# Both mixes of a tile behind the first step of the recurrence, in a kernel of four layers on one core

## The reference

```python
a_t = jnp.tanh(a)
def step(state, x_t):
    state = jnp.tanh(jnp.einsum('bhs,hst->bht', state, a_t) + jnp.einsum('bhd,hds->bhs', x_t, b))
    mixed = jnp.einsum('bhs,hsd->bhd', state, c) + skip[None] * x_t
    return (state, mixed)
...
return tokens + outs @ w_out.T + b_out
```

## Time and profile before

| | |
|---|---|
| median of 3 runs | 2249.52 us (2249.39 to 2250.3) |
| profiled execution: its own time | 2245.83 us |
| profiled execution: span | 2244.1 us |
| PE busy | 2186.6 us, 97% of the span |
| DVE, POOL, ACT busy | 1718.1, 1192.8, 1060.2 us |
| mean granted PE clock | 0.993 |

### The profile page before, as it was taken

The page is one execution under the profiler, slowest core; times in us unless marked ns, Lnnn a source line. Parts: engine busy times, 40 slices in busy tenths (PEclk is TensorE's granted clock), DMA queues, the critical chain, the costliest instruction groups (busy, mean ns, idle before and its releaser), DMA issues.

```text
span 2244.1 us, 92167 instructions
## 1 busy us (share of the span) xinstructions
PE 2186.6 (97%) x37362; PEld 1540.2 (69%) x37362; DVE 1718.1 (77%) x4980; ACT 1060.2 (47%) x2707; POOL 1192.8 (53%) x1680
## 2 busy tenths in 40 slices
PE   9999999999999999999999999998999999999997
PEld 5566565656556555556777777777888888887775
DVE  5788888888887777769999999994555555556997
ACT  4655665656666665552222222222444444443444
POOL 4555555655655555536666666674344444442334
PEclk9999999999999999999999999998999999999999
DMA  4111111211121111111210101100011111111232
GB/s 150 58 49 58 67 63 63 67 58 58 67 67 58 68 58 58 50 52 31 68 33 30 33 31 32 42 24 29 28 33 36 34 33 33 37 49 38 87 94 76
DMA packets 101634, 117.83 MB, mean 53 GB/s; under 512 B 10672, under 2 KB 80080, under 8 KB 101456
## 3 DMA queue, kind: packets, MB, share of 16 engines
q1 hardware_dynamic: 101456, 115.44, 15.8%
HBM read 48.29 MB, written 33.55 MB: 36 GB/s over the span
## 4 chain that ended last, share of the span: by engine, by line
PE 92%; DVE 4%; issue 2%; ACT 1%; POOL 0%; DVEq 0%; ACTq 0%; POOLq 0%
PE ps_state L1734 10%; PE ps_down L1373 7%; PE ps_gate L1366 7%; PE ps_up L1366 7%; PE ps_near L812 6%; PE ps_far L592 5%; PE ps_near L584 5%; PE ps_far L584 4%; PE ps_near L592 3%; PE ps_far L627 3%; PE ps_far L611 3%; PE ps_far L604 3%; PE ps_state L1765 3%; PE ps_state L1737 2%; PE ps_r L2152 2%; PE ps_v L2163 2%
## 5 line engine op out<-in xcount | busy, mean ns | idle before, releaser
L1616 ACT ACTIVATE r_state<-ps_state 128x64 f32<-128x64 f32 x1024 | 228.4, 223 | 288.7 <-PE ps_state L1737 283.9
L1734 PE MATMUL ps_state<-r_state,later_pairs_a 64*64 64x32 f32 x8192 | 338.3, 219 | 24.4 <-ACT r_state L1616 11.7
L1734 PEld LDWEIGHTS ps_state<-r_state,later_pairs_a 64*64 64x64 f32 x8192 | 298.2, 135 | 76.1 <-issue 56.3
L1737 PE MATMUL ps_state<-r_state,later_pairs_a 64*64 64x32 f32 x8192 | 334.8, 220 | 1.2 <-issue 1.1
L480 DVE CUSTOM_DVE_ANT_0 ps_near<-ps_near,mask 128x512 f32<-128x512 f32 (+1 forms) x512 | 270.4, 589 | 83.6 <-PE ps_near L584 83.5
L340 POOL TENSOR_SCALAR_AFFINE_SELECT probsT<-probsT 128x512 f32<-128x512 f32 x256 | 160.6, 640 | 266.1 <-ACT probsT L460 168.2
L1737 PEld LDWEIGHTS ps_state<-r_state,later_pairs_a 64*64 64x64 f32 x8192 | 289.7, 135 | 0.4 <-issue 0.4
L480 DVE CUSTOM_DVE_ANT_0 ps_far<-ps_far,mask 128x384 f32<-128x384 f32 (+1 forms) x512 | 198.3, 457 | 33.6 <-PE ps_far L584 32.5
L1256 POOL TENSOR_TENSOR f_fp<-f_rounded,f_scale 128x960 f32<-128x960 f32 (+2 forms) x67 | 117.3, 1751 | 162.7 <-DVE f_rounded L1345 162.7
L1278 ACT ACTIVATE f_silu<-ps_gate 128x704 f32<-128x704 f32 x64 | 48.4, 757 | 285.8 <-PE ps_gate L1366 285.8
L592 PE MATMUL ps_far<-Q,K 32*128 32x256 f32 (+2 forms) x1536 | 181.2, 416 | 1.2 <-ACT probsT L457 0.5
(11 more groups left out here) (218 smaller groups left out, 5411.7 us busy)
## 6 DMA issues: line engine op xcount, KB each, us to landing
q_swap<-q_sin SPq DMA_DIRECT2D x128, 128.0 KB, 2.1
k_swap<-k_sin SPq DMA_DIRECT2D x128, 128.0 KB, 2.1
xT<-in_xT_dram SPq DMA_DIRECT2D x16, 512.0 KB, 3.7
xtok<-in_x_dram SPq DMA_DIRECT2D x16, 512.0 KB, 3.8
x_rows<-x SPq DMA_DIRECT2D x16, 512.0 KB, 2.9
f_x<-x_rows SPq DMA_DIRECT2D x64, 128.0 KB, 2.1
x_rows<-f_x SPq DMA_DIRECT2D x64, 128.0 KB, 1.8
r_x<-x_rows SPq DMA_DIRECT2D x64, 128.0 KB, 2.1
```

The source lines that it names most:

```text
L1616: nc.scalar.activation(state[:, j % 2, banks, :, t, 0, :], sums[j % 2][:, banks, :, now], ACT.Tanh).then_inc(state_ready[t], 1)
L1734: nc.tensor.matmul(sums[j % 2][half(v), stays, c, now], A[half(v), 3 * q, c, :], last[half(v), stays, c, :], start=False, stop=True, skip_ ...
L1737: out = nc.tensor.matmul(sums[j % 2][half(1 - v), changes, c, now], A[half(v), 3 * q + 1 + was, c, :], last[half(v), changes, c, :], start ...
```

## The change

The table of places has one place for the mixes instead of two. Behind the recurrence of place 1 both mixes are issued, c = 0 and then c = 1; behind that of place 3 nothing is issued. The waits of the first mix stay ahead of both, and each mix still raises `mix_full` by one.

```diff
-        MIXES, PROJECTS, TURNS, FEEDS = (1, 3), (5, 9), 7, (13, 15)
+
+        MIXES, PROJECTS, TURNS, FEEDS = 1, (5, 9), 7, (13, 15)
@@ in slots(t), behind recur(j, t, q, states)
-                    if at in MIXES and not first:
-                        if at == MIXES[0]:
-                            for side in range(SIDES):
-                                await_count(state_ready[STEPS - 1], states[side])
-                        mix(j, MIXES.index(at)).then_inc(mix_full, 1)
+                    if at == MIXES and not first:
+                        for side in range(SIDES):
+                            await_count(state_ready[STEPS - 1], states[side])
+                        for c in range(CC):
+                            mix(j, c).then_inc(mix_full, 1)
```

## The result

The changed kernel takes 2254.45 us, median of 9 runs (2252.11 to 2256.76), against 2247.99 us of the kernel before in as many runs beside it (2244.32 to 2250.3). The ratio is 1.003, with a 95% interval of 1.0019 to 1.004: slower by 6.5 us, where +7.6 us was forecast. The forecast of 2257.1 us stood on the three-run median of 2249.52; nine runs put the kernel before 1.5 us lower. The profiled execution took 2254.45 us, with a span of 2252.7 us against 2244.1.

A forecast was written before the change was run, and what follows sets the result against it. Each step takes the longer of PE's issue work and the 0.86 us round through ACT. Step 0 gains 0.22 us, step 1 loses 0.10: +0.12 a tile, +7.6 us over 63 tiles, 2257.1 us, range 2252.5 to 2261.

The forecast's parts named there:

- Step 0: Recurrence of t = 0 to that of t = 1: grows by the second mix, 0.22 us, to 1.22 us.
- Step 1: Recurrence of t = 1 to that of t = 2: falls from 0.96 to 0.86 us once its mix is gone.
- the round through ACT: Loop bound: one round of PE, ACT and PE for one side, 0.86 us, with 0.83 as low end.
- A saved border: Change between 64*64 and 128*32 tiles on PE: one fewer each way saves 0.26 us of PE's time a tile.
- The sum: From the start of t = 0 to the project: 2.44 us becomes 2.56, +0.12 us a tile, +7.6 us for 63.
- rival 2: The cost drowns, partly by issue waits at tile borders falling into step 1's new wait: 2251 to 2254 us; 10 in 100.
- The start: Tiles 0 to 2: tile 0 unchanged, having no mixes; the next two +0.12 us each, with granted clock and issue waits unchanged.
- rival 3: PE's clock falls for longer: one more half-clock stretch at the start, at most 3.3 us, in range; 1.2 GHz throughout, 2 in 100.
- The array as the bound of step 1: PE's issue work alone sets step 1, 0.48 us: -0.26 us a tile, 2233.1 us, faster; 4 in 100.
- The full cost of a single mix (0.36): In step 0 the second mix costs as much as alone: +0.26 us a tile, 2265.9 us; 3 in 100.

The follow-up runs named there:

- experiment 2: Changed kernel with the second mix not computed, so not the reference's result: 2244.44 us, ratio 0.9984 to the kernel before.
- 3: Changed kernel with four unused 64x64 matmuls on 160 columns in the emptied place 3: 2248.61 us, ratio 1.0005 to the kernel before.
- experiment 4: Changed kernel with one unused 64x64 matmul on 32 columns between the two mixes: 2277.98 us, ratio 1.0125 to the kernel before.
- 1: Changed kernel with both mixes in place 3 instead of place 1: 2255.09 us, ratio 1.0036 to the kernel before.
- 10: Changed kernel with four unused 64x64 matmuls on 256 columns in the emptied place 3: 2251.33 us, ratio 1.0020 to the kernel before.
- 9: Kernel before with two unused 64x64 matmuls on 128 columns in its empty place 11: 2250.85 us, ratio 1.0023.
- 6: Kernel before with four unused 64x64 matmuls on 96 columns in its empty place 11: 2261.15 us, ratio 1.0055.
- 7: Kernel before with four tiles to a round of the hardware loop instead of two: 2696.58 us, ratio 1.1993.
- 5: Changed kernel with its projects cut by columns over places 3, 5 and 9: 2272.78 us, ratio 1.0106 to the kernel before.

## Why the prediction was right

**The bounds and the place of the cost** were right. Step 0 grew by the second mix, 0.58 less 0.36 = 0.22 us as in the earlier trace rows. Step 1 fell to the round through ACT, 0.87 us measured in the tile shown and 0.86 forecast; experiments 2 and 3 show each by itself. A saved border counts only where PE is the bound, and it is real (experiment 4).

**The sum** was 0.12 us a tile, and 0.098 was measured in the loop. Up to the project a tile grew by 0.10 to 0.11 us (2.55 against 2.44 in the tiles shown, 0.12 forecast), as step 1 took 0.87 us for the 0.86 forecast and the recurrence ahead of the project 0.46 for 0.48. Two terms were reckoned at nothing and nearly cancel. Behind the project a tile is 0.03 us longer. At the loop's branch it is 0.03 us shorter on average: before, three tiles of 7.79 or 7.80 us follow one of 7.55; changed, 7.89 and 7.78 take turns. The wait at step 1 didn't swallow these pauses; this is rival 2's effect in small, at the head of the tile and not where I looked. That gives 5.9 us for 60 tiles, and 6.2 for 63.

**The start** was wrong. Tiles 0 to 2 were to cost 0.12 us each like the others, and the recorded text said that the clock stays as it is, and that it is wrong if clock or issue waits move by more than 3 us. In two profiles of each kernel the stretch from the first recurrence to tile 3 is 3.8 us longer in the changed one, and its time at half clock went from 13.7 and 17.1 us to 27.3 and 20.5; the issue pauses in it, 5.6 and 5.2 us before and 6.6 and 7.8 changed, grew by less. So rival 3, a clock that falls for longer, is there, though how the 3.8 us split between clock and pauses isn't shown. In the loop the clock stayed at 1.00, as forecast.

**How good the number is.** The measured median is inside the range, at the low edge of the forecast's own 2254.5 to 2260. The pairs of profiled executions differ by 8.6 and 10.4 us (the second pair ran on two chips), the medians by 6.5 (4.3 to 9.0 by the interval). Next to a loop that costs 6 us the medians leave little for the start, so the 3.8 us needn't be there in every execution; two profiles of each can't tell. The forecast's 7.6 us lie between a loop that came out lower and a start that came out higher, and that they agree so well with 6.5 is partly luck.

**The rivals.** The array as the bound of step 1 was refuted by the 116 waits and by experiment 2. The full cost of a single mix (0.36) wasn't paid. The cost didn't drown: the interval of the ratio, 1.0019 to 1.0040, lies above 1.

## What to carry to other kernels

In a recurrence that goes round two engines, each step takes the longer of the round and of what stands in it, so filler is free only up to the round (here there is room for 0.38 us beside 0.48 us of PE; some 0.30 cost nothing and 0.47 cost its step 0.08); two pieces in one step leave the next one's shadow unused, even if they save a change of tile mode. Price a move by what the step that takes it grows by and what the step that loses it falls by, each against the round, and not by the piece's own duration. No version here that computes the reference beats the kernel before.

## What the runs showed that was not expected

**Unused work made the kernel faster.** The changed kernel with place 3 filled (3) is at 2248.61 us, 5.8 us under the changed one without it (ratios to before of 1.0005 and 1.0030); only 1.5 us of this are in the loop. The stretch from the first recurrence to tile 3 shows the rest. It goes roughly with how much of steps 0 to 2 PE fills: 48.2 us with one mix left out (2), 46.4 and 46.4 changed, 45.3 with the pair in place 3 (1), 42.5 and 42.7 before, 41.1 and 42.3 with place 3 filled (3, 10) and 40.2 with the border (4). The time at half clock in it goes much the same way: 30.7 us, then 27.3 and 20.5, 20.5, 13.7 and 17.1, 13.7 and 10.2, and 13.7. That the clock makes the difference is the likely reading, but no run varied the work in tiles 0 to 2 alone, and work in place 11 (9) brought nothing (43.3 us, with 13.7 at half clock); the cause stays open.

**More instructions in the loop's body can be dear.** Four small matmuls and a wait more in each tile brought 9 more instruction loads and some 18 us in half of the runs (6); a body of twice the length brought 450 us (7). A tile has 180 fp32 matmuls in two passes, each pass with a weight load, so 720 instructions: an estimate of 1440 for two tiles and 2880 for four. The Trainium skill (Runtime: NRT & Kernel Launch, Instruction fetch mechanics) says that PE's buffer holds 2048 instructions, refilled in blocks of 256, and that a taken branch whose target isn't in the current window of two blocks waits for a fetch. The 2048 fit 7, but a window of two blocks, 512 instructions by these figures (an estimate), is not what these traces show: in the kernel before the instruction queue that grew in 6 and 7 (q8) has no packet from 1568 to 2035 us, while its body of 1440 goes round 30 times. Nor does length alone explain 6 and 5, by the same count at 1472 and 1504 instructions with 122 loads each: the changed kernel with place 3 filled (3, 10) has 1472 too and kept its 113. What sets them apart stays open.
